# Attention B's norm turned by DMA instead of by TensorE

## The chip, the cores and the metric

The kernel runs on one core of a Trainium2 chip. TensorE (PE in the profile) does matmuls and, with an identity matrix, transposes; VectorE (DVE), ScalarE (ACT) and GpSimd (POOL) do element-wise work; SyncE (SP) issues DMAs, and a DMA can transpose 16-bit data on its way. The engines run side by side and wait for each other on semaphores. The metric is the time of one execution in microseconds (us) on the device; of several runs the median.

## The reference

Four residual layers follow each other on 1024 rows of 512 numbers (two sequences of 512): attention A, a mixture-of-experts FFN, attention B, and the same FFN again. Cut to what matters:

```
x = hidden_states                                  # 2 x 512 x 512
x = x + attn_a(layernorm(x), quantised weights)
x = x + ffn(layernorm(x), gate_w, lora_A, lora_B)
x = x + attn_b(layernorm(x), Wq, Wk, Wv, Wo)
x = x + ffn(layernorm(x), gate_w, lora_A, lora_B)

layernorm(x) = (x - mean(x)) / sqrt(var(x) + eps)
attn_b: q = n @ Wq (32 heads of 16), k = n @ Wk, v = n @ Wv (8 heads of 16),
        rotary embedding of q and k, causal softmax, out @ Wo
```

## The kernel before, in words

The 1024 rows are NT = 8 tiles of 128 rows. All matmuls are made from 16-bit pairs: a value is a high part (its f16 rounding) and a low part (the rest), and a product is three matmuls (high by high, high by low, low by high; `three`, L1253 to L1255). A projection contracts over the 512 columns, so it needs the normalised rows turned: `xt` holds, for each tile, four 128x128 blocks of the high part and four of the low part, columns on the partitions.

A norm of tile t has these steps. DVE takes the statistics (`ln_stats`), POOL the reciprocal root (`ln_rsqrt`, L591), DVE subtracts and scales (`ln_norm`, L1861). From there two ways exist. In the norms of attention A and B (c = 0 and 2) the result goes to `xn`, PE turns it with four f32 transposes into a PSUM bank (`ln_t`, L1262), ACT makes the high part out of the bank (`ln_hi`, L889) and DVE the low part (`ln_lo`, L1871), both straight into `xt`. In the norms of the FFNs (c = 1 and 3) `ln_norm` writes a PSUM bank in row layout, ACT writes the high part and DVE the low part into `rows` (`row_hi`, L897; `row_lo`, L1866; two buffers), and SP turns both with one DMA transpose of 128 x 1024 (`turn_rows`, L500), whose landing PE awaits on `d_rows`.

The work around the change is the projection stage of attention B. The order on every engine is written out by hand. The engines' queues go strictly in order, SP's among them: an instruction that waits holds all behind it. PE does, for t from 0 to 5, the query projection of tile t (`project_q`, 12 matmuls of 512 columns), the transposes of tile t + 2, and the key and value projection (`project_kv`, 12 matmuls of 256 columns); tiles 6 and 7 are cut in halves with the first scores between them. Behind a query projection come, in this order, the rotary products on DVE (`rope_q`, L2267 and L2268), their sum on POOL (`queries_rot`, L819), the high part into `q_stack` on ACT (L1215), the low part on POOL (`queries_low`, L830), and SP's DMA transpose into `qt_b` (`turn_queries`, L519). Keys go the same way with half the columns: products (`rope_k`), sum (`keys_rot`, L824), high part (L1221), low part (`keys_low`, L813), transpose into `kt_b` (`turn_keys`, L523). POOL's order for a tile is `queries_rot(t)`, `keys_low(t - 1)`, `keys_rot(t)`, `queries_low(t)`: the keys' low part of a tile stands behind the sum of the next tile's queries. SP issues the turn of tile t's queries and then that of its keys, behind a wait for `stacks_set`, which POOL sets when it has cleared the stacks (its last memset is L806).

In front of the stage lies the FFN's second half: PE's `second(m)` (12 matmuls of 512 columns per tile), DVE's addition and statistics (`y_stats`), and ACT's and POOL's preparation of attention B's weights (`w_scale` L1140, `w_high` L1144, `w_low` L746; `b_o` is the last).

Of the kernel before, what the change touches and what calls it, by code (L numbers as in the profile page):

```python
# [24 lines left out]
P = 128  # L25
B, S, D = 2, 512, 512
TOK = B * S
NT = TOK // P
ST = S // P
KT = D // P  # L30
# [71 lines left out]

LN_BANK = {0: (0, 1, 0, 1, 6, 1, 6, 6), 2: (2, 3, 2, 3, 2, 3, 2, 3)}
XN_BANK = {1: (3, 2), 3: (4, 3)}

HALF = NT // 2
GATE_BANK = [(7, 4), (5, 2)]
# [102 lines left out]
def build(nc, t_in, out):  # L212
    ctx = ExitStack()
    with ctx:
# [7 lines left out]
        bank = [banks[:, i] for i in range(8)]  # L222
# [5 lines left out]
        xn = sb("xn", [P, 2, D], F32)  # L228
# [187 lines left out]
        d_turned, d_rows = ([sem(f"{n}{i}") for i in range(2)] for n in ("d_turned", "d_rows"))  # L416
# [43 lines left out]

        def rows_landed(c, t):

            return 16 * (HALF * (c // 2) + t // 2 + 1)

        block = ctx.enter_context(nc.Block())
        N_CONST = 3
# [3 lines left out]
        def _(sp):  # L470
# [43 lines left out]
                turn_rows(1, t)  # L514
            for t in range(NT):
                turn_hidden(0, t)
            def turn_queries(t):
                sp.wait_ge(bq_lo, t + 1)
                sp.dma_start_transpose(qt_b[:, :, t * P:(t + 1) * P], q_stack[:, t % 2]).then_inc(d_q[t % 2], 16)  # L519
# [5 lines left out]
            def turn_max(q, c):  # L525
                sp.wait_ge(bsplit_done, 2 * q + c + 1)
                if q >= 2:
                    sp.wait_ge(d_mrows[c][q % 2], 32 * (q // 2))
                sp.dma_start_transpose(m_turned[:, q % 2, c].rearrange("p (i n) -> p i n", n=P),
                                       m_stack[:, q % 2, c].rearrange("p i n -> p (i n)")).then_inc(d_mturn[c], 16)  # L530

# [8 lines left out]

            sp.wait_ge(stacks_set, 2)
            for t in range(NT - 2):
                turn_queries(t)
                turn_keys(t)
            turn_max(0, 0)
# [339 lines left out]
        @block.scalar  # L885
        def _(act):
            def ln_hi(c, t):
                act.wait_ge(xt_ps, NT * (c // 2) + t + 1)
                act.activation(xt_hi[:, :, t * P:(t + 1) * P],  # L889
                               bank[LN_BANK[c][t]][:].rearrange("p (k n) -> p k n", k=KT),  # L890
                               ACT.Copy, scale=X_UP).then_inc(xthi_done, 1)

            def row_hi(c, t):
                act.wait_ge(xn_ready, NT * c + t + 1)
                if c == 3 or t >= 2:
                    act.wait_ge(d_rows[t % 2], rows_landed(c, t) - 16)
                act.activation(rows[:, t % 2, 0], bank[XN_BANK[c][t % 2]][:], ACT.Copy, scale=X_UP).then_inc(xthi_done, 1)  # L897

# [284 lines left out]
            def experts(ph):  # L1183
                c = 1 + 2 * ph
                for t in range(3):
                    h_out(ph, t)
                    row_hi(c, 5 + t)
                h_out(ph, 3)
                gate_exp(ph, 0)
                h_out(ph, 4)  # L1190
                h_out(ph, 5)
                rows_high(ph, 0)
                h_out(ph, 6)
                rows_high(ph, 1)
                gate_exp(ph, 1)
                h_out(ph, NT - 1)
                for t in range(2, NT):
                    rows_high(ph, t)
                    if ph == 0:
                        w, n = beside[t - 2]  # L1200
                        w(n)

            experts(0)

# [15 lines left out]
                rk = rk1[:, i2].rearrange("p (h d) -> p h d", d=B_HD).unsqueeze(2)  # L1220
                act.activation(st[:, :, :, 0], rk.broadcast_to([P, KV_HEADS, 4, B_HD]), ACT.Copy).then_inc(bk_hi, 1)  # L1221

            ln_hi(2, 0)
            ln_hi(2, 1)
            for t in range(NT):
                if t + 2 < NT:
                    ln_hi(2, t + 2)
                stack_high(t)

            for q in range(SETS + 2):  # L1230
# [19 lines left out]
        def _(pe):  # L1250
# [6 lines left out]
            def ln_t(c, t):  # L1257
                pe.wait_ge(xn_ready, NT * c + t + 1)
                if t >= 2:
                    pe.wait_ge(xt_done, NT * c + t - (c > 0 or t != NT - 1))  # L1260
                for k in range(KT):
                    mm = pe.transpose(bank[LN_BANK[c][t]][:, k * P:(k + 1) * P],  # L1262
                                      xn[:, t % 2, k * P:(k + 1) * P], ident[:])
                mm.then_inc(xt_ps, 1)

# [311 lines left out]
            def experts(ph):  # L1577
                c = 1 + 2 * ph
                m0, f0 = ph * 2 * NT, ph * NT
                if ph == 0:  # L1580
                    pe.wait_ge(wlo_done, 5)
                    pe.wait_ge(o_added, NT * (KV_HEADS - 1) + 3)
                for t in range(NT):
                    if t == NT - 1 and ph == 0:
                        pe.wait_ge(redw[1], 3)
                        pe.transpose(bank[PEAK_BANK][:, P:P + 3], w_peaks[0:3], ident[0:3, 0:3]).then_inc(redw[1], 1)
                    pe.wait_ge(d_rows[t % 2], rows_landed(c, t))
                    if t == 1 and ph == 0:
                        pe.wait_ge(o_added, NT * (KV_HEADS - 1) + 6)
                    if t == NT - 3 and ph == 0:  # L1590
                        pe.wait_ge(amaxw_done[1], 3)
                        pe.transpose(bank[PEAK_BANK][0:3, 0:P], amax_w[:, 3:6], ident[:]).then_inc(redw[1], 1)
                    if t == HALF:
                        if ph == 0:
                            pe.wait_ge(o_added, NT * KV_HEADS)
                        else:
                            pe.wait_ge(y_added, 2 * NT)
                    e0 = t % HALF * EXPERTS
                    wide(bank[GATE_BANK[ph][t // HALF]][:, e0:e0 + EXPERTS], t, "gate", EXPERTS).then_inc(g_ps, 1)
                    if t >= 2:  # L1600
                        pe.wait_ge(h_done, f0 + t - 1)
                    wide(bank[t % 2][:], t, "lora_a", D).then_inc(h_ps, 1)
                if ph == 0:
                    pe.wait_ge(wlo_done, 9)
                for t in range(NT):
                    if ph == 0 and t == NT - 1:
                        ln_t(2, 0)
                    second(m0 + t, "lora_b")
                if ph == 0:
                    ln_t(2, 1)  # L1610

            experts(0)

# [57 lines left out]
            def project_q(t, first=True, last=True):  # L1671


                if first:
                    pe.wait_ge(xt_done, 2 * NT + t + 1)
                    if t >= 2:
                        pe.wait_ge(bq_mul, t - 1)
                mm = wide(bank[t % 2][:], t, "b_q", D, range(0 if first else KT // 2, KT if last else KT // 2))
                if last:
                    mm.then_inc(bq_ps, 1)  # L1680
# [7 lines left out]

            for t in range(NT - 2):
                project_q(t)  # L1690
                ln_t(2, t + 2)
                project_kv(t)
            pe.wait_ge(zeros_done, 5)
            project_q(NT - 2, last=False)
# [134 lines left out]
        def _(dve):  # L1829
# [22 lines left out]

            def ln_norm(c, t):
                i = NT * c + t
                if c % 2:
                    dve.wait_ge(xt_done, i - 1)
                elif t >= 2:
                    dve.wait_ge(xt_ps, NT * (c // 2) + t - 1)
                dve.wait_ge(ln_rstd, i + 1)
                to = bank[XN_BANK[c][t % 2]][:] if c % 2 else xn[:, t % 2]  # L1860
                dve.tensor_scalar(to, x[:, t], mv[:, t, 0:1], rstd[:, t:t + 1], ALU.subtract,  # L1861
                                  ALU.mult).then_inc(xn_ready, 1)

# [5 lines left out]
            def ln_lo(c, t):  # L1869
                dve.wait_ge(xthi_done, NT * c + t + 1)  # L1870
                dve.scalar_tensor_tensor(out=xt_lo[:, :, t * P:(t + 1) * P],  # L1871
                                         in0=bank[LN_BANK[c][t]][:].rearrange("p (k n) -> p k n", k=KT),
                                         scalar=X_UP, in1=xt_hi[:, :, t * P:(t + 1) * P], op0=ALU.mult,
                                         op1=ALU.subtract).then_inc(xt_done, 1)

# [352 lines left out]
            def experts(ph):  # L2228
# [10 lines left out]
                for t in range(NT):  # L2239
                    if t + 3 < NT:  # L2240
                        rows_low(ph, t + 3)
                    if ph:
                        y_add(m0 + t, t, c_ffn)
                        continue
                    if t == NT - 1:
                        ln_norm(2, 1)
                        ln_lo(2, 0)
                        ln_norm(2, 2)
                        ln_lo(2, 1)
                    y_stats(m0 + t, t, c_ffn, 2)  # L2250
                    if t == NT - 3:
                        ln_norm(2, 0)

            experts(0)
# [67 lines left out]
            for t in range(NT - 2):  # L2322
                rope_q(t)
                rope_k(t)
                ln_lo(2, t + 2)
                if t + 3 < NT:
                    ln_norm(2, t + 3)
            b_max(0, 0, 3)
# [148 lines left out]
```

## Time and profile before

| | us |
|---|---|
| runs | 952.43, 947.94, 952.37 |
| median | 952.37 |
| profiled execution, its own time | 950.79 |
| span of the profile in it | 949.1 |

| engine | busy us | share |
|---|---|---|
| PE | 912.1 | 96% |
| DVE | 771.8 | 81% |
| ACT | 598.8 | 63% |
| POOL | 618.9 | 65% |

The span runs from the first to the last instruction; the rest of the execution's time (1.7 us) lies around it. The stage of this case is from about 716 to 755 us of the span. A start time is counted from the span's start. A timeline row of the trace gives start, duration, engine, line, operation, output and inputs, count, and in brackets how long the engine had been idle and who released it.

### The profile page before, as it was taken

The numbers are of one execution on the slowest core, as the hardware profiler recorded it, in microseconds if no ns is written. First come the engines' busy times: TensorE is split into PE (matmuls) and PEld (weight loads), VectorE is DVE, ScalarE is ACT, GpSimd is POOL, SyncE is SP. The second block draws the span as 40 slices with busy tenths as digits, with TensorE's granted clock in tenths as the row PEclk, the third lists the DMA queues.
The fourth block names the chain that finished last, engine by engine and source line by source line (L and its number), as shares of the span: only waits on it lengthen the run. The fifth ranks groups of instructions, "written<-read, shape, count | busy, mean of one in ns | idle before, by whom it ended". The sixth has DMA issues, their size and how long they took to land.

```text
span 949.1 us, 19791 instructions
## 1 busy us (share of the span) xinstructions
PE 912.1 (96%) x6698; PEld 487.6 (51%) x6698; DVE 771.8 (81%) x1812; ACT 598.8 (63%) x1323; POOL 618.9 (65%) x668
## 2 busy tenths in 40 slices
PE   5889999999999999999999999999999989999998
PEld 3445555555555555545555555554445534444543
DVE  6888887887887788788788878898878879996764
ACT  4677666676667567666576756646463469997331
POOL 4788876968777687687777777822368744553211
PEclk9999999999999999999999999999999999999999
DMA  9177376484665556647557465464332943121145
GB/s 339 51 182 173 87 185 145 63 211 107 122 186 88 144 116 157 144 86 199 117 101 190 83 144 144 87 175 84 76 82 55 163 80 64 42 43 24 23 86 159
DMA packets 256005, 114.10 MB, mean 120 GB/s; under 512 B 244144, under 2 KB 244784, under 8 KB 251312
## 3 DMA queue, kind: packets, MB, share of 16 engines
q1 hardware_dynamic: 246416, 70.42, 39.1%
q10 hardware_dynamic: 9504, 42.49, 12.9%
q8 instruction: 60, 0.98, 0.4%
q14 instruction: 25, 0.20, 0.1%
HBM read 49.84 MB, written 2.10 MB: 55 GB/s over the span
## 4 chain that ended last, share of the span: by engine, by line
PE 76%; DVE 10%; ACT 6%; issue 3%; DMA 3%; POOL 1%; SPq 1%; ACTq 0%; DVEq 0%; POOLq 0%
PE bank L1253 16%; PE bank L1255 16%; PE bank L1254 16%; PE bank L1734 4%; PE bank L1352 3%; PE bank L1354 3%; PE bank L1353 3%; PE bank L1372 3%; PE bank L1374 3%; PE bank L1373 3%; ACT bank L989 2%; PE bank L1666 2%; DVE bw_hi L1981 2%; DVE bank L1964 2%; PE bank L1640 2%
## 5 line engine op out<-in xcount | busy, mean ns | idle before, releaser
L622 POOL TENSOR_TENSOR rt<-rt 128x512 f32<-128x512 f32 x80 | 101.6, 1273 | 131.8 <-DVE rt L1949 131.8
L1981 DVE SCALAR_TENSOR_TENSOR bw_hi<-bank,rden,bw_hi 128x128 f16<-128x128 f32 (+3 forms) x256 | 123.3, 544 | 60.9 <-ACT bw_hi L1025 60.9
L989 ACT ACTIVATE bank<-bank,shift,c_score 128x128 f32<-128x128 f32 (+3 forms) x256 | 147.3, 605 | 2.1
L1964 DVE CUSTOM_DVE_ANT_0 bank<-bank,mask_w 128x512 f32<-128x512 f32 (+3 forms) x256 | 117.9, 520 | 21.5 <-PE bank L1354 21.5
L1025 ACT ACTIVATE bw_hi<-bank,rden 128x128 f16<-128x128 f32 (+3 forms) x256 | 114.5, 535 | 22.4 <-DVE rden L1974 22.2
L984 ACT ACTIVATE shift<-smax,c_score 128x4 f32<-128x4 f32 x64 | 19.0, 297 | 155.4 <-DVE smax L1964 155.4
L629 POOL TENSOR_TENSOR arena<-rt,arena 128x512 f16<-128x512 f32 x80 | 92.4, 1158 | 8.6 <-ACT arena L973 7.8
L1253 PE MATMUL bank<-xt,wq_hi 128*128 128x512 f16 x256 | 97.0, 379 | 0.0
L1254 PE MATMUL bank<-xt,wq_hi 128*128 128x512 f16 x256 | 97.0, 379 | 0.0
L1255 PE MATMUL bank<-xt,wq_lo 128*128 128x512 f16 x256 | 97.0, 379 | 0.0
L1253 PE MATMUL bank<-wo_hi,arena 128*128 128x512 f16 x256 | 97.0, 379 | 0.0
L1254 PE MATMUL bank<-wo_lo,arena 128*128 128x512 f16 x256 | 97.0, 379 | 0.0
L1255 PE MATMUL bank<-wo_hi,arena 128*128 128x512 f16 x256 | 97.0, 379 | 0.0
L1006 ACT ACTIVATE pt<-bank,c_score_b 128x512 f32<-128x512 f32 x128 | 79.6, 684 | 15.2 <-PE bank L1666 13.1
L1352 PE MATMUL bank<-arena 128*128 128x512 f16 (+3 forms) x256 | 73.4, 300 | 7.1 <-DVE bw_hi L1981 6.8
L1372 PE MATMUL bank<-bw_lo,arena 128*128 128x512 f16 (+3 forms) x256 | 76.6, 299 | 1.9 <-DMA bw_lo<-bw_hi 1.4
L1373 PE MATMUL bank<-bw_lo,arena 128*128 128x512 f16 (+3 forms) x256 | 76.6, 299 | 0.0
L1353 PE MATMUL bank<-arena 128*128 128x512 f16 (+3 forms) x256 | 76.6, 299 | 0.0
L1354 PE MATMUL bank<-arena 128*128 128x512 f16 (+3 forms) x256 | 73.8, 299 | 0.0
L1374 PE MATMUL bank<-bw_lo,arena 128*128 128x512 f16 (+3 forms) x256 | 73.3, 299 | 0.0
L1947 DVE TENSOR_TENSOR rt<-bank,sin_a 64x512 f32<-64x512 f32 x80 | 55.5, 693 | 16.6 <-PE bank L1255 14.7
L973 ACT ACTIVATE arena<-rt 128x512 f16<-128x512 f32 x80 | 51.3, 645 | 9.9 <-POOL rt L622 9.9
(241 smaller groups left out, 2453.6 us busy)
## 6 DMA issues: line engine op xcount, KB each, us to landing
qcode<-in_q_codes ACTq DMA_DIRECT2D x7, 1024.0 KB, 5.0
qscale<-in_q_scales ACTq DMA_DIRECT2D x7, 1024.0 KB, 7.2
ocode<-in_o_codes ACTq DMA_DIRECT2D x7, 1024.0 KB, 4.9
oscale<-in_o_scales ACTq DMA_DIRECT2D x7, 1024.0 KB, 7.9
kvcode<-in_k_codes ACTq DMA_DIRECT2D x8, 256.0 KB, 7.5
kvcode<-in_v_codes ACTq DMA_DIRECT2D x8, 256.0 KB, 7.9
kvscale<-in_k_scales ACTq DMA_DIRECT2D x8, 256.0 KB, 8.1
kvscale<-in_v_scales ACTq DMA_DIRECT2D x8, 256.0 KB, 8.9
```

What stands on the lines that cost most here:

```text
L989: act.activation(a_rows(i, s), a_rows(i, s), ACT.Exp, bias=shift[:, s % 2, c:c + 1], scale=c_score[:, 0:1], accum_out=bank[3][:, SUMS_AT + ...
L1025: act.activation(p_row[:, s % 2, HI_AT[i]:HI_AT[i] + P_STEP * i + 1:P_STEP], turned_back(i, s), ACT.Copy, scale=rden[:, s % 2, c:c + 1]).t ...
L1253: pe.matmul(out_ap, a_hi, b_hi, start=(k == 0), stop=False)
L1254: pe.matmul(out_ap, a_hi, b_lo, start=False, stop=False)
L1255: return pe.matmul(out_ap, a_lo, b_hi, start=False, stop=(stop and k == n - 1))
L1352: pe.matmul(o_ap, q_hi[:, s, qs], k_hi[:, b, 0:w], start=True, stop=False)
L1353: pe.matmul(o_ap, q_hi[:, s, qs], k_lo[:, b, 0:w], start=False, stop=False)
L1354: mm = pe.matmul(o_ap, q_lo[:, s, qs], k_hi[:, b, 0:w], start=False, stop=True)
L1372: pe.matmul(o_ap, v_hi[:, b, vs], hi, start=(kt == 0), stop=False)
L1373: pe.matmul(o_ap, v_hi[:, b, vs], lo, start=False, stop=False)
L1964: dve.tensor_tensor_reduce(bank[bk][:, o:o + (i + 1) * P], bank[bk][:, o:o + (i + 1) * P], mask_w[:, S - (i + 1) * P:S], 1.0, LOWEST, ALU. ...
L1981: dve.scalar_tensor_tensor(out=p_row[:, s % 2, LO_AT[i]:LO_AT[i] + P_STEP * i + 1:P_STEP], in0=turned_back(i, s), scalar=rden[:, s % 2, c: ...
```

## The change

Attention B's norm (c = 2) goes the way of the FFNs' norms. `ln_norm(2, t)` writes a PSUM bank in row layout, `row_hi` and `row_lo` fill `rows`, SP's `turn_rows(2, t)` turns them into `xt`, and `project_q(t)` waits for `d_rows`. PE's eight calls of `ln_t(2, t)` are gone. In the FFN's tail the first norms move: `ln_norm(2, 0)` one tile earlier, the low parts of tiles 0 and 1 before tiles 6 and 7's statistics, and ACT makes the high part of tile 0 between `rows_high(7)` and the last weight step. On SP tiles 0 and 1 are turned after the FFN's last hidden turn, tile 2 behind the wait for `stacks_set`, and tile t + 2 ahead of the queries and keys of tile t.

```diff
-LN_BANK = {0: (0, 1, 0, 1, 6, 1, 6, 6), 2: (2, 3, 2, 3, 2, 3, 2, 3)}
-XN_BANK = {1: (3, 2), 3: (4, 3)}
+LN_BANK = (0, 1, 0, 1, 6, 1, 6, 6)
+XN_BANK = {1: (3, 2), 2: (2, 3), 3: (4, 3)}
@@ SyncE
+            turn_rows(2, 0)
+            turn_rows(2, 1)
...
                 if q >= 2:
                     sp.wait_ge(d_mrows[c][q % 2], 32 * (q // 2))
+                elif c == 0:
+                    sp.wait_ge(d_rows[q], rows_landed(2, NT - 2 + q))
...
             sp.wait_ge(stacks_set, 2)
             for t in range(NT - 2):
+                turn_rows(2, t + 2)
                 turn_queries(t)
                 turn_keys(t)
@@ ScalarE, FFN tail and attention B
                     if ph == 0:
+                        if t == NT - 1:
+                            row_hi(2, 0)
                         w, n = beside[t - 2]
                         w(n)
+                if ph == 0:
+                    row_hi(2, 1)
...
-            ln_hi(2, 0)
-            ln_hi(2, 1)
             for t in range(NT):
                 if t + 2 < NT:
-                    ln_hi(2, t + 2)
+                    row_hi(2, t + 2)
                 stack_high(t)
@@ TensorE
                 for t in range(NT):
-                    if ph == 0 and t == NT - 1:
-                        ln_t(2, 0)
                     second(m0 + t, "lora_b")
-                if ph == 0:
-                    ln_t(2, 1)
...
                 if first:
-                    pe.wait_ge(xt_done, 2 * NT + t + 1)
+                    pe.wait_ge(d_rows[t % 2], rows_landed(2, t))
...
             for t in range(NT - 2):
                 project_q(t)
-                ln_t(2, t + 2)
                 project_kv(t)
@@ VectorE
+                    if t == NT - 2:
+                        row_lo(2, 0)
+                        ln_norm(2, 1)
                     if t == NT - 1:
-                        ln_norm(2, 1)
-                        ln_lo(2, 0)
                         ln_norm(2, 2)
-                        ln_lo(2, 1)
+                        row_lo(2, 1)
                     y_stats(m0 + t, t, c_ffn, 2)
-                    if t == NT - 3:
+                    if t == NT - 4:
                         ln_norm(2, 0)
...
                 rope_q(t)
                 rope_k(t)
-                ln_lo(2, t + 2)
+                row_lo(2, t + 2)
                 if t + 3 < NT:
                     ln_norm(2, t + 3)
```

SP's queue at the start of the stage before; `qt_b<-q_stack` turns a tile's queries, `kt_b<-mt` its keys, `mt<-m_stack` is the FFN's hidden turn.

```order
L500 DMA_TRANSPOSE xt<-rows 128x8x128 x8
L510 DMA_TRANSPOSE mt<-m_stack 128x8x128 x8
L519 DMA_TRANSPOSE qt_b<-q_stack 128x16x128
L523 DMA_TRANSPOSE kt_b<-mt 128x8x128
L519 DMA_TRANSPOSE qt_b<-q_stack 128x16x128
L523 DMA_TRANSPOSE kt_b<-mt 128x8x128
```

The same place of SP's queue after the change; `xt<-rows` behind the hidden turns are the new ones.

```order
L500 DMA_TRANSPOSE xt<-rows 128x8x128 x8
L510 DMA_TRANSPOSE mt<-m_stack 128x8x128 x8
L500 DMA_TRANSPOSE xt<-rows 128x8x128 x3
L521 DMA_TRANSPOSE qt_b<-q_stack 128x16x128
L525 DMA_TRANSPOSE kt_b<-mt 128x8x128
L500 DMA_TRANSPOSE xt<-rows 128x8x128
L521 DMA_TRANSPOSE qt_b<-q_stack 128x16x128
L525 DMA_TRANSPOSE kt_b<-mt 128x8x128
```

Tiles 0 to 2 now go ahead of the first queries, and tiles 3 to 7 each stand behind the keys of the tile three below.

ScalarE at the end of the FFN and the start of the stage, before (`bw_hi<-oscale` is the high part of the weight `b_o`, `bv` the values of a tile):

```order
L1172 ACTIVATE m_stack<-hs 128x512
L1144 ACTIVATE bw_hi<-oscale 128x2048
L889 ACTIVATE xt<-bank 128x4x128 x3
L1208 ACTIVATE bv<-bank 128x8x16
L1215 ACTIVATE q_stack<-rq 128x32x32
```

The same place after:

```order
L1177 ACTIVATE m_stack<-hs 128x512
L902 ACTIVATE rows<-bank 128x512
L1149 ACTIVATE bw_hi<-oscale 128x2048
L902 ACTIVATE rows<-bank 128x512 x2
L1217 ACTIVATE bv<-bank 128x8x16
L1224 ACTIVATE q_stack<-rq 128x32x32
```

The first of attention B's high parts now stands ahead of the weight's high part, which so waits for the first norm.

## Rows read from the trace of the kernel before

**Rows 1.** The page: the span, and the shares of the last chain.
```profile
span 949.1 us, 19791 instructions
...
PE 76%; DVE 10%; ACT 6%; issue 3%; DMA 3%; POOL 1%; SPq 1%; ACTq 0%; DVEq 0%; POOLq 0%
```

**Rows 2.** Chain that ended last, 690 to 780 us: start, us, what.
```profile
693.74 2.70 DMA mt<-m_stack
...
740.46 0.44 PE bank L1262 x4
...
755.14 0.48 DVE rq L2267 x2
```

**Rows 3.** PE's timeline: second half's start, then query projections of tiles 3, 4, 5, 7.
```profile
696.57 0.38 PE L1253 MATMUL bank<-lora_b_hi,mt 128*128 128x512 f16 x1 [1.98 <-DMA mt<-m_stack]
...
733.37 0.38 PE L1253 MATMUL bank<-bw_hi,xt 128*128 128x512 f16 x1
...
737.71 0.38 PE L1253 MATMUL bank<-bw_hi,xt 128*128 128x512 f16 x1
...
742.05 0.38 PE L1253 MATMUL bank<-bw_hi,xt 128*128 128x512 f16 x1
...
751.86 0.39 PE L1253 MATMUL bank<-bw_hi,xt 128*128 128x512 f16 x1
```

**Rows 4.** SP's timeline, turns of queries 0, keys 0, queries 1, keys 4.
```profile
729.29 2.02 SPq L519 DMA_TRANSPOSE qt_b<-q_stack  x1
731.36 1.64 SPq L523 DMA_TRANSPOSE kt_b<-mt  x1
733.05 1.82 SPq L519 DMA_TRANSPOSE qt_b<-q_stack  x1
...
748.19 1.24 SPq L523 DMA_TRANSPOSE kt_b<-mt  x1
```

**Rows 5.** POOL's timeline: last memset; then sum of queries 5, keys 4, queries 5.
```profile
725.35 0.31 POOL L806 MEMSET mt<- 128x256 f32 x1
...
746.27 1.26 POOL L819 TENSOR_TENSOR rq<-rq 128x512 f32<-128x512 f32 x1 [0.72 <-DVE rq L2268]
747.50 0.67 POOL L813 TENSOR_TENSOR mt<-hs,mt 128x256 f16<-128x256 f32 x1
...
748.70 1.16 POOL L830 TENSOR_TENSOR q_stack<-rq,q_stack 128x512 f16<-128x512 f32 x1
```

**Rows 6.** DMA from 729 to 752 us: queue's packets, MB, share; issues with us to landing.
```profile
q1 hardware_dynamic: 16397, 4.12, 100.8%
...
qt_b<-q_stack SPq DMA_TRANSPOSE x6, 4.5
kt_b<-mt SPq DMA_TRANSPOSE x5, 3.5
```

**Rows 7.** Line L500, all sixteen row turns of the FFNs' norms: issue ns, landing us.
```profile
L500 SPq DMA_TRANSPOSE xt<-rows x16: 1231/1233/1369, 662.1 to 914.9; - x16
...
DMA to landing us min/median/max: 3.0/3.1/4.8
```

**Rows 8.** Windows: us, busy of PE, PEld, DVE, ACT, POOL, PEclk, DMA share, GB/s.
```profile
697.00:700.60 3.60, 3.60 (x10) 1.27 (x9) 1.82 (x5) 3.60 (x4) 1.04 (x1) 0.53 0.42 94
700.60:704.00 3.40, 3.40 (x17) 1.57 (x16) 2.85 (x5) 2.43 (x4) 2.56 (x3) 1.00 0.34 77
```

**Rows 9.** Lines L1861, L897, L1866 from 655 to 700 us: ns min/median/max.
```profile
L1861 DVE TENSOR_SCALAR bank<-x,mv,rstd x8: 805/810/815, 659.9 to 683.1; 128x512 f32<-128x512 f32 x8
...
L897 ACT ACTIVATE rows<-bank x8: 597/597/598, 660.7 to 684.6; 128x512 f16<-128x512 f32 x8
...
L1866 DVE SCALAR_TENSOR_TENSOR rows<-bank,rows x8: 682/688/692, 661.4 to 685.3; 128x512 f16<-128x512 f32 x8
```

**Rows 10.** Timelines of DVE and ACT in the FFN's tail.
```profile
714.13 0.15 DVE L1851 TENSOR_SCALAR mv<-mv 128x1 f32<-128x1 f32 x1
...
710.09 1.89 ACT L1144 ACTIVATE bw_hi<-oscale 128x2048 f16<-128x2048 f32 x1
```

More of the change, by code:

```diff
@@ L461, in rows_landed @@
         def rows_landed(c, t):
-            return 16 * (HALF * (c // 2) + t // 2 + 1)
+            return 16 * (HALF * (c - 1) + t // 2 + 1)
         block = ctx.enter_context(nc.Block())
@@ L887, in ln_hi @@
             def ln_hi(c, t):
-                act.wait_ge(xt_ps, NT * (c // 2) + t + 1)
+                act.wait_ge(xt_ps, t + 1)
                 act.activation(xt_hi[:, :, t * P:(t + 1) * P],
-                               bank[LN_BANK[c][t]][:].rearrange("p (k n) -> p k n", k=KT),
+                               bank[LN_BANK[t]][:].rearrange("p (k n) -> p k n", k=KT),
                                ACT.Copy, scale=X_UP).then_inc(xthi_done, 1)
@@ L894, in row_hi @@
                 act.wait_ge(xn_ready, NT * c + t + 1)
-                if c == 3 or t >= 2:
+                if c > 1 or t >= 2:
                     act.wait_ge(d_rows[t % 2], rows_landed(c, t) - 16)
@@ L1261, in ln_t @@
                 for k in range(KT):
-                    mm = pe.transpose(bank[LN_BANK[c][t]][:, k * P:(k + 1) * P],
+                    mm = pe.transpose(bank[LN_BANK[t]][:, k * P:(k + 1) * P],
                                       xn[:, t % 2, k * P:(k + 1) * P], ident[:])
@@ L1854, in ln_norm @@
                 i = NT * c + t
-                if c % 2:
+                if c:
                     dve.wait_ge(xt_done, i - 1)
                 elif t >= 2:
-                    dve.wait_ge(xt_ps, NT * (c // 2) + t - 1)
+                    dve.wait_ge(xt_ps, t - 1)
                 dve.wait_ge(ln_rstd, i + 1)
-                to = bank[XN_BANK[c][t % 2]][:] if c % 2 else xn[:, t % 2]
+                to = bank[XN_BANK[c][t % 2]][:] if c else xn[:, t % 2]
                 dve.tensor_scalar(to, x[:, t], mv[:, t, 0:1], rstd[:, t:t + 1], ALU.subtract,
@@ L1871, in ln_lo @@
                 dve.scalar_tensor_tensor(out=xt_lo[:, :, t * P:(t + 1) * P],
-                                         in0=bank[LN_BANK[c][t]][:].rearrange("p (k n) -> p k n", k=KT),
+                                         in0=bank[LN_BANK[t]][:].rearrange("p (k n) -> p k n", k=KT),
                                          scalar=X_UP, in1=xt_hi[:, :, t * P:(t + 1) * P], op0=ALU.mult,
```

## The prediction

> **What bounds the kernel now.** I read the page first. PE makes 76% of the chain that ended last [rows 1], so the kernel is bound by TensorE over its whole length, and what counts in one stage is what PE waits for there. The chain in the stretch of the change shows that: it goes through PE's matmuls of the projections without a break, the four transposes of each tile are in it with 0.44 us [rows 2], and it passes to DVE at 755.14, after the last query projection. PE's timeline gives the beat: the query projections of tiles 3, 4 and 5 start at 733.37, 737.71 and 742.05, 4.34 us apart, and that of tile 7 at 751.86 [rows 3]. Without its transposes a tile would take PE 4.34 - 0.44 = 3.90. I call S(t) the start of tile t's query projection, and compare S(7) before and after: all that follows (scores, maxima, softmax) hangs on it.
>
> The second resource is the queue that receives new work. SP turns a tile's queries in 2.02 or 1.82 us and its keys in 1.64, back to back at the start [rows 4], about 3.7 of the 4.34. From 729 to 752 us that queue's packets fill all 16 DMA engines (100.8% of them, 4.12 MB in 23 us) [rows 6]. This is a stage in which DMA has almost nothing to spare, and the change puts 5 more transposes between those of queries and keys.
>
> **What the change removes.** 32 f32 transposes on PE, eight times 0.44 = 3.5 us, all in the chain. ACT's and DVE's two steps stay one for one at about the same cost (0.60 and 0.69 us in the FFN's form [rows 9]), and the norm into PSUM takes 0.81; DVE and ACT have idle time in the stage (DVE is released by PE in each tile), so I take nothing for them. The bounds for that are 0 and, if DVE's fell into the chain, 0.1 a tile.
>
> **The start of the stage.** The statistics of tile 4 end at 714.13 + 0.15 = 714.3 [rows 10]. The norm of tile 0 follows (0.8), then ACT's high part (0.6, ready 715.7), while DVE does tile 5's addition and statistics (1.8, to 716.9); the low part is done at 717.5, SP turns, and it lands 3.1 later [rows 7] at 720.6. S(0) was 720.1, so 0.5 later, though PE is ready a microsecond earlier. ACT's high part of `b_o` (1.89 us) began at 710.09 [rows 10] and now stands behind the first row part: it ends near 717.5 instead of 712, and POOL's low parts of it, its last three reciprocal roots and memsets end some 0.3 us later than 725.35 + 0.31 [rows 5], near 726.0. That releases tile 2's turn, so S(2) = 726.0 + 3.1 = 729.1, as before within 0.1. The first queries are ready 0.3 later too. Up to here nothing is won or lost.
>
> **Tile 3, where the wait begins.** Queries 0 were turned at 729.29, keys 0 at 731.36 and queries 1 at 733.05 [rows 4]; with 0.3 more the third place is free at 733.35, and there tile 3's rows are turned, though they have been ready since about 730.6. A 256 KB transpose behind another lands after 3.5 us here (the keys' median; the rows' own median in quiet stretches is 3.1) [rows 6, 7], and PE starts 0.13 after a landing (693.74 + 2.70 to 696.57) [rows 2, 3]. S(3) = 733.35 + 3.5 + 0.13 = 737.0, against 733.37 before. PE has finished tile 2 at 729.1 + 3.9 = 733.0 and stands still for 4 us.
>
> **The loop over tiles.** Tile t + 3's rows are issued behind tile t's keys. Those keys wait for POOL's `keys_low(t)`, which stands behind `queries_rot(t + 1)`, which needs the query projection of tile t + 1. Before, from S(5) = 742.05 the sum of queries 5 ran at 746.27, the keys' low part of tile 4 at 747.50, and SP issued keys 4 at 748.19 [rows 3, 4, 5]: 6.14 us. So S(t + 3) = S(t + 1) + 6.14 + 1.24 (the keys' issue) + 3.2 (landing, between 3.1 and 3.5) + 0.13 = S(t + 1) + 10.7, that is 5.35 us a tile instead of 4.34. A second bound is the queue itself: 3.7 + 1.23 [rows 7] = 4.9 a tile. The loop is the tighter. With the clock full: S(4) = 741.8 (rows issued at 738.15 behind queries 1 and keys 1), S(5) = 737.0 + 10.7 = 747.7, S(6) = 752.5, S(7) = 758.4. Against 751.86 that is +6.6.
>
> **PE's clock.** After the idle 1.98 us before 696.57 the granted clock in 697.0 to 700.6 was 0.53, half speed, and 1.00 behind it [rows 3, 8]; 3.6 x 0.47 = 1.7 us of PE's work was lost. The Trainium skill says the same of a matmul loop that waits for DMAs ("TensorE: Matmul & The Clock Gate", section on HAM oscillation): each such wait can send the array to half clock again. That rule speaks for a loss at every long wait; by it the stage would pay twice. The idle times ahead of S(3) (4 us) and S(5) (about 3) are both longer than the 1.98 that sufficed. I take one spell, 1.7 us, since the wait before S(5) shrinks by what S(4) is late; the bounds are 0 and 3.4. It delays query 3's end and so keys 2 and S(5), S(7): on the path. Sum: 950.8 (the profiled execution's own time) + 6.6 + 1.7 = 959.1. The median of the three runs is 1.6 above the profiled execution, by which it would be 960.7; I say 960.
>
> A rule of the Trainium skill speaks against the queue as a bound. "DMA: Bandwidth & Descriptors", Specifications, gives the fabric a ceiling of 435 GB/s; an estimate from it for the 1.05 MB of queries, keys and rows is 2.4 us a tile, so the rows would cost nothing in bandwidth. The trace disagrees for transposes: at a full share it moved 4.12 MB in 23 us, 180 GB/s, and one 256 KB turn holds the queue 1.23 us, 213 GB/s. No number above uses the rule.
>
> **Rivals.**
> - *Faster: PE sets the beat.* If SP reached each row turn before PE needed it, each tile would take 3.9 and the 3.5 us would be won: 950.8 - 3.7 = 947.1. The point from which it decides: tile 3's rows must be issued by 729.4, that is before queries 0 or right behind them. For it speaks that rows are ready 2 us earlier than SP comes to them; against it that the order on SP is fixed and that queries 0 and keys 0 hold the queue until 733.
> - *Only the queue's capacity counts.* If keys were ready when SP comes to them, rows would follow each other by 4.9: the issue of tile 7's is 733.35 + 4 x 4.9 = 753.0, S(7) = 756.6, +4.7, 955.5. Against it speak the 6.14 us from a projection to the keys' issue, measured without any wait of SP before it.
> - *One wait, then hidden.* The wait before S(3) costs 3.6 and later tiles run at 3.9, so that 4 x 0.44 comes back: +1.9, 952.7, no difference. It needs the loop to be shorter than 7.8 us for two tiles, and the three rows that make it give 10.7.
> - *Two or more clock spells*, 962.5 and above.
>
> **How the numbers follow.** The loop with one or two spells, or none: 0.70 (957.4 to 962.5), more than that 0.05, the queue's capacity alone 0.13, hidden again 0.06, faster 0.06. A change of under 0.5% (4.8 us) can't be told from none in measurements of this kernel. Against the median 952.4, slower by more than that is from 957.1: the first two cases and a part of the third, 0.80; same 0.14; faster 0.06. The range of 8 in 10 is 954.5 to 964.
>
> **What would show it.** Right: after the third turn of the stage SP's timeline reads rows, queries, keys in turn; PE's largest releaser in the stage is the DMA `xt<-rows`, with some 4 us before tile 3's projection and PE idle at tile 5; a period near 5.3 for tiles 3 to 7; S(7) near 758 to 760; a stretch of half clock after S(3); everything behind tile 7 shifted alike. Wrong: S(3) at 733 would refute the queue order's role; a period of 4.9 with SP never idle would put the queue's capacity in the loop's place; waits on PE elsewhere (bank or statistics) would mean another bound.

## The result, and the profile after

| | before | after |
|---|---|---|
| median of the runs, us | 952.4 | 962.75 |
| lowest to highest, us | 947.94 to 952.58 | 961.75 to 964.93 |
| profiled execution, us | 950.79 | 964.93 |
| span of the profile, us | 949.1 | 963.2 |

The kernel before has four runs here, a fourth of 952.58 beside the three above. The changed kernel is slower, by a ratio of 1.0113 with a 95% interval of 1.0093 to 1.0133. The page after, first PE's busy time, then the shares of the last chain and its costliest lines:

```profile
PE 917.1 (95%) x6666; PEld 487.5 (51%) x6666; DVE 772.9 (80%) x1812; ACT 599.2 (62%) x1323; POOL 616.8 (64%) x668
...
PE 74%; DVE 13%; ACT 5%; DMA 3%; issue 3%; SPq 1%; ACTq 0%; POOL 0%; DVEq 0%; POOLq 0%
PE bank L1260 15%; PE bank L1261 15%; PE bank L1262 15%; PE bank L1736 4%; PE bank L1359 3%; PE bank L1361 3%; PE bank L1360 3%; PE bank L1379 3%; PE bank L1381 3%; PE bank L1380 3%; PE bank L1643 2%; ACT bank L994 2%; PE bank L1669 2%; DMA xt<-rows 2%; DVE bw_hi L1983 2%
```

PE has 32 instructions fewer (6698 before) and is busy 5 us longer, because more of them ran at half clock (mean granted clock of the execution 0.984, before 0.995); and the landing of `xt<-rows` has come into the chain with 2%, beside the shares before in [rows 1].

The profiled executions can't be subtracted as they stand. SP's first hidden turn, in front of everything that the change touches, was at 693.74 before [rows 2] and is at 698.84 after:

```profile
698.84 20.00 SPq L510 DMA_TRANSPOSE mt<-m_stack  x8
```

These 5.1 us lie in identical instructions. In the traces of all the kernels of this study that moment lies between 693.63 and 698.84, so it varies from run to run. I therefore count inside the stage, from the query projection of tile 2. PE's timeline after, query projections of tiles 2 to 7 (start, us, engine, line, operation, idle time before it and who ended it):

```profile
734.15 0.39 PE L1260 MATMUL bank<-bw_hi,xt 128*128 128x512 f16 x1 [0.26 <-DMA xt<-rows]
...
741.76 0.61 PE L1260 MATMUL bank<-bw_hi,xt 128*128 128x512 f16 x1 [3.54 <-DMA xt<-rows]
...
748.40 0.38 PE L1260 MATMUL bank<-bw_hi,xt 128*128 128x512 f16 x1
...
755.75 0.39 PE L1260 MATMUL bank<-bw_hi,xt 128*128 128x512 f16 x1 [3.28 <-DMA xt<-rows]
...
761.09 0.38 PE L1260 MATMUL bank<-bw_hi,xt 128*128 128x512 f16 x1 [1.27 <-issue]
...
766.61 0.39 PE L1260 MATMUL bank<-bw_hi,xt 128*128 128x512 f16 x1
```

The same start of tile 2 before, to which tiles 3, 4, 5 and 7 of [rows 3] belong:

```profile
729.04 0.38 PE L1253 MATMUL bank<-bw_hi,xt 128*128 128x512 f16 x1
```

From tile 2's projection to tile 7's it was 751.86 - 729.04 = 22.82 us before and is 766.61 - 734.15 = 32.46 after: 9.64 more, which is the measured difference of the medians (10.35) but for 0.7. Two long waits for row turns, 3.54 and 3.28 us, lie in it. SP's timeline says why they are there; rows of tile 3, rows, queries and keys around tiles 4 to 7, after:

```profile
738.12 1.34 SPq L500 DMA_TRANSPOSE xt<-rows  x1
...
743.54 1.33 SPq L500 DMA_TRANSPOSE xt<-rows  x1
744.91 2.15 SPq L521 DMA_TRANSPOSE qt_b<-q_stack  x1
750.46 1.89 SPq L525 DMA_TRANSPOSE kt_b<-mt  x1
752.39 1.31 SPq L500 DMA_TRANSPOSE xt<-rows  x1
...
757.58 1.34 SPq L500 DMA_TRANSPOSE xt<-rows  x1
...
763.18 1.34 SPq L500 DMA_TRANSPOSE xt<-rows  x1
```

Tile 3's rows were complete at 735.07 (DVE's low part) and turned at 738.12. Between 747.06 and 750.46 SP waits for tile 2's keys, and tile 5's rows stand behind them. POOL's timeline shows that these keys were ready just when SP issued them, and only after an idle time of 6.57 us in which POOL waited for tile 3's rotary products:

```profile
748.53 1.26 POOL L824 TENSOR_TENSOR rq<-rq 128x512 f32<-128x512 f32 x1 [6.57 <-DVE rq L2271]
749.76 0.67 POOL L818 TENSOR_TENSOR mt<-hs,mt 128x256 f16<-128x256 f32 x1
```

The windows around tile 3's wait give the clock (last three numbers: granted clock, DMA share, GB/s; a granted clock of 1.00 is 2.4 GHz, one of 0.50 is 1.2 GHz):

```profile
736.00:740.50 4.50, 2.22 (x17) 1.37 (x14) 3.18 (x8) 2.87 (x5) 3.89 (x6) 1.00 1.10 205
740.50:747.30 6.80, 5.54 (x15) 2.11 (x16) 0.20 (x1) 1.44 (x3) 1.33 (x2) 0.50 1.05 194
747.30:750.00 2.70, 2.70 (x19) 1.75 (x18) 2.55 (x8) 0.44 (x2) 1.47 (x2) 0.99 0.59 110
```

TensorE has half speed for 6.8 us, from the idle time into tile 3's projection, which with its keys and values takes 748.40 - 741.76 = 6.64 us instead of 3.9. The slow projection is also what made tile 2's keys late: they were issued 750.46 - 741.76 = 8.70 us after the start of tile 3's projection, where the same step took 6.14 before.

### The profile page after: what moved, and what is told of

It is laid out like the page before. It is cut to its first block, busy times and chain, and to the rows that moved or that the text cites. A ratio compares the mean times of both kernels' runs of the same rounds, so it can differ in the third digit from the quotient of the medians.

```text
span 963.2 us, 19741 instructions
## 1 busy us (share of the span) xinstructions
PE 917.1 (95%) x6666; PEld 487.5 (51%) x6666; DVE 772.9 (80%) x1812; ACT 599.2 (62%) x1323; POOL 616.8 (64%) x668
## 4 chain that ended last, share of the span: by engine, by line
PE 74%; DVE 13%; ACT 5%; DMA 3%; issue 3%; SPq 1%; ACTq 0%; POOL 0%; DVEq 0%; POOLq 0%
PE bank L1260 15%; PE bank L1261 15%; PE bank L1262 15%; PE bank L1736 4%; PE bank L1359 3%; PE bank L1361 3%; PE bank L1360 3%; PE bank L1379 3%; PE bank L1381 3%; PE bank L1380 3%; PE bank L1643 2%; ACT bank L994 2%; PE bank L1669 2%; DMA xt<-rows 2%; DVE bw_hi L1983 2%
```

## The experiments

"Tile 2 to 7" is the time from tile 2's query projection to tile 7's; "turn to turn" is the mean distance of neighbouring row turns on SP, from the first that stands behind a tile's keys. Both are read in one profiled execution of each kernel; the medians are of 4 to 10 executions. The lengthening of "tile 2 to 7" and that of the median agree within 2.5 us, so the medians alone don't tell kernels 1 or 2 us apart. Each kernel ran beside the kernel before (medians 951.1 to 952.3).

| kernel | tile 2 to 7 | turn to turn | median us | ratio to before, 95% interval |
|---|---|---|---|---|
| before | 22.82 | | 952.4 | 1 |
| after | 32.46 | 6.27 | 962.75 | 1.0093 to 1.0133 |
| rows ahead | 30.63 | 5.56 | 959.12 | 1.0043 to 1.0096 |
| keys early | 29.89 | 5.46 | 957.65 | 1.0047 to 1.0088 |
| kept busy | 30.76 | 5.85 | 958.31 | 1.0036 to 1.0079 |
| three by DMA | 22.81 | | 950.74 | 0.9972 to 1.0005 |
| rows ahead + keys early | 30.27 | 5.55 | 957.39 | 1.0044 to 1.0087 |
| rows ahead, half the bytes | 28.16 | 5.40 | 957.37 | 1.0042 to 1.0098 |
| keys early, half the bytes | 28.43 | 5.38 | 956.63 | 1.0037 to 1.0065 |
| keys early, kept busy | 29.58 | 5.49 | 955.89 | 1.0032 to 1.0061 |
| keys early, two turns | 35.09 | 6.66 | 964.99 | 1.0086 to 1.0155 |
| five by DMA | 28.68 | | 955.53 | 1.0018 to 1.0054 |
| four by DMA, ahead | 24.52 | | 952.09 | 0.9983 to 1.0014 |

**Rows ahead of queries on SP.**

```diff
             sp.wait_ge(stacks_set, 2)
+            turn_rows(2, 2)
             for t in range(NT - 2):
-                turn_rows(2, t + 2)
+                if t + 3 < NT:
+                    turn_rows(2, t + 3)
                 turn_queries(t)
                 turn_keys(t)
```

> Edit: on SyncE tile t+3's rows are turned ahead of the queries and keys of tile t, instead of behind them (tile 2's still first). Bytes and instructions are those of the changed kernel. Theory A (the place in SyncE's order makes the wait: rows that are ready stand behind keys that wait for the next tile's projection, and the long waits halve TensorE's clock): no wait of more than 1 us before tile 3's projection, no stretch of half clock in the stage, tile spacing set by the queue's 4.9 us at most, tile 7's projection 1.5 to 3 us later than in the kernel before instead of 9.6; in all 953.5 to 956. Rival B (the DMA engines' capacity for the added bytes makes all of the loss): the same bytes cost the same, 961 to 964. Rival C (the loss comes from DVE's and ACT's new order in the FFN's tail): unchanged, 961 to 964.

Tile 3's wait was gone, as expected, and with it the fall of the clock there. But the time came down by 3.6 us and not by 8: 959.1, outside the expectation, with tile 7's projection 7.8 us later than before and not 1.5 to 3. SP's timeline of this kernel is without a gap, and its turns are longer (five of six queries' turns took 2.15 to 3.31 us; in the kernel before five of the six took 1.82 to 2.02 and one 3.21):

```profile
736.04 1.34 SPq L500 DMA_TRANSPOSE xt<-rows  x1
737.42 1.81 SPq L521 DMA_TRANSPOSE qt_b<-q_stack  x1
739.28 1.90 SPq L525 DMA_TRANSPOSE kt_b<-mt  x1
741.22 1.34 SPq L500 DMA_TRANSPOSE xt<-rows  x1
742.60 3.31 SPq L521 DMA_TRANSPOSE qt_b<-q_stack  x1
745.96 1.34 SPq L525 DMA_TRANSPOSE kt_b<-mt  x1
747.35 1.32 SPq L500 DMA_TRANSPOSE xt<-rows  x1
```

The expectation also left out that the scores need the keys, which come out of the same full queue: the first scores waited for those of tile 3. The granted clock fell there, to 0.50 from 755.5 to 758.5, where no spell at all was expected.

```profile
754.92 0.39 PE L1645 MATMUL bank<-kt_b,qt_b 64*128 64x512 f16 x2 [2.49 <-DMA kt_b<-mt]
```

Tile 6's projection, which stands ahead of these scores, started 21.02 us after tile 2's (17.34 before, 26.94 in the changed kernel); so of the 7.8 us that were left, 3.7 had arisen by then and 4.1 arose between tiles 6 and 7. Theory A, that the order makes the loss by itself, fell here. Rival B, that capacity makes all of it, didn't hold either, since 3.6 us did come back.

**Keys' low part early on POOL.**

```diff
                 queries_rot(t)
-                if t:
-                    keys_low(t - 1)
                 if t == NT - 1:
+                    keys_low(t - 1)
                     b_split(0, 1)
...
                 queries_low(t)
+                if t < NT - 2:
+                    keys_low(t)
```

> Edit: on GpSimd the low part of tile t's keys (tiles 0 to 5) is made right behind tile t's queries' low part, instead of behind the sum of tile t+1's queries. SyncE's order is that of the changed kernel. Theory A says the loop rows(t+1) - projection(t+1) - keys low(t) - rows(t+3) is cut at the keys: tile 3 still waits (some 3.5 us, its rows stand behind queries 0 and keys 0) and the clock still falls there, but tile 5 doesn't wait any more (under 1 us) and tile 7's projection comes about 2.5 us earlier than in the changed kernel: 959 to 961. Rival B (capacity alone): no difference, 961.5 to 964.

Tile 7 came 2.57 us earlier, as expected, and the median is lower than expected (957.65 against 959 to 961). A wait of 2.05 us before tile 5 remained, where under 1 was expected: with the loop cut the turns follow each other without a gap, at 5.46 us a tile. The clock behaved otherwise than expected too: after tile 3's wait of 3.31 us it stayed at 1.00, and it fell to 0.50 from 748.5 to 751.5, after the wait of 2.05. So the 2.57 us hold two things, the loop that was cut and a spell of half clock that moved; the last of the runs with TensorE kept busy takes them apart.

**PE kept busy while it waits.**

```diff
                 if first:
+                    keep_busy(CTX_BANK, {3: 22, 4: 6, 5: 10, 6: 5}.get(t, 0))
                     pe.wait_ge(d_rows[t % 2], rows_landed(2, t))
```

> Edit: TensorE runs idle matmuls (128x384, into a bank that nobody reads) ahead of its wait for the rows of tiles 3, 4, 5 and 6 (22, 6, 10 and 5 of them), so that it waits busy. Everything else is the changed kernel. Theory A with the clock as a cost of its own: the granted clock stays 1.00 in the stage, projection of tile 3 and its keys and values take 3.9 us and not 6.6, the waits for rows stay at the same places, tile 7's projection starts 3 us earlier: 959 to 960.5. Rival (the clock's loss is hidden behind the rows' wait anyway): 962 to 963.

The granted clock was 1.00 over the whole stage (window 735 to 762), and 958.3 is below the changed kernel by 4.4 us and below the expectation. Inside the stage only 1.7 us came back, not 3: the faster projection of tile 3 runs into tile 4's rows (a wait of 1.79 us), which wait for the queue. The idle matmuls have a price too: tile 5's rows, turned at 744.43, landed 3.3 us later, at 747.7, and its projection began at 749.07, behind the ten matmuls. So the clock is a cost of its own, in part hidden behind the turns; in the stage it is worth 1.7 us at least, and about a microsecond more if that delay is counted.

```profile
735.00:762.00 27.00, 24.73 (x173) 13.75 (x172) 14.53 (x35) 10.12 (x17) 14.64 (x19) 1.00 1.03 180
```

```profile
747.44 1.79 PE L1277 MATMUL bank<-mask_w 128*128 128x384 bf16 x10
749.07 0.38 PE L1260 MATMUL bank<-bw_hi,xt 128*128 128x512 f16 x1
```

With tile 3's projection at full clock, SP did not wait for tile 2's keys. They were ready at 742.82, 6.1 us after the start of that projection, and SP came to them at 743.07, behind a queries' turn of 3.24 us; behind one of 2 us it would have waited for about one. SP's first wait for keys (1.8 us) came with tile 3's.

```profile
739.79 3.24 SPq L521 DMA_TRANSPOSE qt_b<-q_stack  x1
743.07 1.31 SPq L525 DMA_TRANSPOSE kt_b<-mt  x1
```

**Only tiles 0 to 2 by DMA.**

```diff
+BY_DMA = 3
@@ SyncE
-                turn_rows(2, t + 2)
+                if t + 2 < BY_DMA:
+                    turn_rows(2, t + 2)
@@ TensorE
                 project_q(t)
+                if t + 2 >= BY_DMA:
+                    ln_t(2, t + 2)
                 project_kv(t)
```

(ACT, DVE and the waits take the matching way per tile.)

> Edit: only the norms of tiles 0, 1 and 2 are turned by DMA; tiles 3 to 7 are turned by TensorE as in the kernel before. Part of the change is undone, so five of the eight row transposes are gone from SyncE's order between queries and keys, and five of TensorE's are back. Theory A: all of the loss lies in tiles 3 to 7, so tile 3's projection starts at the time of the kernel before (within 0.3 us) and the time is that of before, 951 to 953.5. Rival C (the loss, or part of it, comes from the FFN's tail, where DVE's and ACT's order changed and the weight's high part waits): 954 or more.

It took 22.81 us from tile 2 to tile 7, that of before to 0.01. The median, 950.74, is 0.3 below the range and can't be told from that of before. So the FFN's tail, the start of the stage and the first three turns cost nothing, which refutes rival C, and gain nothing that these runs can tell. The rows of tiles 2 and 7:

```profile
733.23 0.38 PE L1265 MATMUL bank<-bw_hi,xt 128*128 128x512 f16 x1
...
756.04 0.39 PE L1265 MATMUL bank<-bw_hi,xt 128*128 128x512 f16 x1
```

**Rows ahead and keys early together.** The edit is the sum of the two diffs.

> Edit: both of the two earlier ones together: SyncE turns tile t+3's rows ahead of tile t's queries and keys, and GpSimd makes the keys' low part right behind the queries'. No waiting order is left that keeps a turn back; the bytes are all there. Theory D (formed from the runs before: with the order mended the queue of transposes itself is full, at some 5.45 us for a tile's rows, queries and keys, and that sets the beat): row turns 5.3 to 5.6 apart on average, SyncE's queue without idle time, the first scores still wait for the keys of tile 3, and the time is that of either edit alone, 957 to 959.5. Theory A (order alone makes the loss): with both edits no wait is left and the time comes to 953 to 955.

The median is 957.4, as theory D has it, and no better than the better of the two alone. SP has next to no idle time and rows still follow each other by 5.55. The first scores still wait 1.97 us for the keys of tile 3, and the granted clock fell twice, behind the wait of 2.05 us before tile 5 and behind that one. With the order mended the queue, with the spells that its waits bring, is what is left.

**Half the bytes, in two orders.**

```diff
+            def turn_high(c, t):
+                sp.wait_ge(xt_done, NT * c + t + 1)
+                sp.dma_start_transpose(xt[:, 0, :, t * P:(t + 1) * P],
+                                       rows[:, t % 2, 0]).then_inc(d_rows[t % 2], 16)
```

> Edit: rows ahead on SyncE as before, and of tiles 3 to 7 only the high part (128x512, 128 KB) is turned; attention B's low part of these tiles is left as the FFN's norm wrote it, so part of the computation is left out. Instructions and waits are the same, the added bytes of these five turns are halved. Theory D (bytes through the queue): the beat falls by about 0.6 us a tile, to 4.8, row turns 4.6 to 5.0 apart, and tile 7's projection comes 2.5 to 3.5 us earlier than with rows ahead alone: 955 to 957. Rival E (a turn costs a fixed time in the queue whatever its size): no difference, 958.5 to 960.

> Edit: the keys' low part early on GpSimd, SyncE's order of the changed kernel, and of tiles 3 to 7 only the high part turned (the low part is left out as in the other run of this kind). Theory D (bytes through the queue): row turns 4.6 to 5.0 apart instead of 5.46, tile 7's projection 2.5 to 3.5 us earlier than with the full bytes: 954 to 956. Rival E (fixed time for each turn): no difference from the keys' edit alone, 957 to 958.5. Tile 3 still waits some 3 us in both, since its place in the order is the same.

Theory D missed in both: the distance of row turns fell from 5.56 to 5.40 and from 5.46 to 5.38, not to 4.6 to 5.0. Rival E, no difference, is nearer but not exact: tile 7 came 2.5 and 1.5 us earlier, and the medians, 957.4 and 956.6, lie between the two expectations, 1.8 and 1.0 below those with the full bytes, with runs that overlap. Rows landed after 2.6 us instead of 3.4, which is a part of that; another is that both kernels with the full bytes had a spell of half clock in the stage and both with half the bytes none. So bytes are a small part. What holds the queue shows in SP's timeline and DMA's windows of "keys early, half the bytes": a turn of 128 KB keeps SP 1.27 us, nearly what 256 KB do (1.34), and some 2 us behind its start the DMA engines have little to do for half a microsecond or a whole one (last two numbers: DMA share, GB/s).

```profile
733.29 1.27 SPq L505 DMA_TRANSPOSE xt<-rows  x1
734.61 1.85 SPq L526 DMA_TRANSPOSE qt_b<-q_stack  x1
736.51 1.90 SPq L530 DMA_TRANSPOSE kt_b<-mt  x1
738.45 1.27 SPq L505 DMA_TRANSPOSE xt<-rows  x1
```

```profile
735.00:735.50 0.50, 0.00 (x0) 0.00 (x0) 0.34 (x1) 0.00 (x0) 0.50 (x2) 1.00 0.45 91
735.50:736.00 0.50, 0.10 (x1) 0.11 (x2) 0.00 (x0) 0.44 (x1) 0.44 (x2) 1.00 0.19 38
...
740.50:741.00 0.50, 0.00 (x0) 0.00 (x0) 0.50 (x2) 0.28 (x1) 0.50 (x1) 1.00 0.00 0
```

**Keys early and PE kept busy.** Both diffs, with 22, 6, 8 and 5 idle matmuls.

> Edit: the keys' low part early on GpSimd, and idle matmuls on TensorE ahead of its waits for the rows of tiles 3 to 6 (22, 6, 8 and 5 of them). Theory D with the clock as a cost of its own: the clock stays at 1.00 in the stage, the beat is that of the queue, tile 7's projection 28.5 to 29.5 us after tile 2's (29.9 with the keys' edit alone), and the runs lie closer together, 956 to 957.5. Rival (the clock's spells are a cost on top of the queue's beat even with the keys' edit): 954.5 to 956.

Tile 2 to 7 took 29.58 us, just above the range, with row turns 5.49 apart. The median, 955.89, lies 0.1 below theory D's range and in the rival's (954.5 to 956). The runs lie closer together, as expected (953.9 to 957.3, where "keys early" spread from 955.5 to 960.7). The clock's remaining spells are worth between 0.3 us (by the traces) and 1.8 (by the medians), which these runs can't tell apart.

Four kernels now differ in just two things, the keys' early low part and TensorE kept busy. In the time from tile 2 to 7, the early keys are worth 32.46 - 29.89 = 2.57 us where the clock is free to fall, but 30.76 - 29.58 = 1.18 where TensorE is kept busy; the clock is worth 1.70 with the loop and 0.31 without. So about half of what the loop seemed to cost was the slow projection of tile 3, which makes tile 2's keys late. (Each number is of one profile, and the idle matmuls delayed tile 5 in both kept-busy kernels.) With both causes gone 29.58 - 22.82 = 6.8 of the 9.64 us are still there: tile 3's first wait and the queue's beat.

**The same bytes in two turns.**

```diff
+            def turn_parts(c, t):
+                sp.wait_ge(xt_done, NT * c + t + 1)
+                for i in range(2):
+                    sp.dma_start_transpose(xt[:, i, :, t * P:(t + 1) * P],
+                                           rows[:, t % 2, i]).then_inc(d_rows[t % 2], 16)
...
-                turn_rows(2, t + 2)
+                (turn_parts if t else turn_rows)(2, t + 2)
```

> Edit: on top of the keys' early low part, the rows of tiles 3 to 7 are turned by two transposes each, one of the high part and one of the low part (128 KB each), instead of one of 256 KB. The bytes are the same, the turns five more. Theory F (from the run with half the bytes, whose turns still took SyncE 1.27 us each: a transpose holds SyncE's queue some 1.25 us however small it is, so the beat counts turns as well as bytes): row turns of neighbouring tiles 6.4 to 6.9 us apart instead of 5.46, tile 7's projection 34 to 36 us after tile 2's (29.9 without), 962 to 965. Rival D (only bytes count): no difference from the keys' edit alone, 956.5 to 959.

All is as theory F has it: 6.66 us between tiles, 35.09 from tile 2 to 7, 965.0. Five turns more with the same bytes cost 7.3 us against "keys early" in the medians and 5.2 from tile 2 to 7. A rival, that the DMA engines themselves are full, doesn't fit: from 733 to 757 us their share was 108% in "keys early", 98% with half the bytes and 91% here, where the beat was longest. SP's timeline, each row being two turns:

```profile
735.87 2.58 SPq L507 DMA_TRANSPOSE xt<-rows  x2
742.34 2.58 SPq L507 DMA_TRANSPOSE xt<-rows  x2
748.78 3.38 SPq L507 DMA_TRANSPOSE xt<-rows  x2
756.05 2.59 SPq L507 DMA_TRANSPOSE xt<-rows  x2
762.49 2.58 SPq L507 DMA_TRANSPOSE xt<-rows  x2
```

**Five tiles by DMA.** `BY_DMA = 5`.

> Edit: tiles 0 to 4 are turned by DMA, tiles 5 to 7 by TensorE; SyncE's order of the changed kernel for those that are left. Theory (each row turn between queries and keys costs once the queue is behind; what a wait took isn't given back): tile 3 waits some 3.3 us as in the changed kernel, the clock may fall there (0 to 2.7), tile 4 comes 1 to 1.5 us later still at full clock, and from tile 5 on the beat is the 4.34 of before; tile 7's projection 4.3 to 7.5 us later than in the kernel before: 955.5 to 958.5. Rival (the loss comes from the steady state of all tiles alone, and TensorE makes good an early wait): under 2 us, 951 to 953.

Tile 7 came 5.86 us late, in the range, at 955.5, the lower edge. Tile 3 waited as in the changed kernel, its projection ran at half clock, and neither loss is given back, though from tile 4 on the beat is again 4.34:

```profile
737.30 0.61 PE L1265 MATMUL bank<-bw_hi,xt 128*128 128x512 f16 x1 [3.41 <-DMA xt<-rows]
```

**Four tiles by DMA, all ahead.** `BY_DMA = 4`, and `turn_rows(2, 2)` and `turn_rows(2, 3)` in front of the loop.

> Edit: tiles 0 to 3 are turned by DMA, all four before the first queries, tiles 4 to 7 by TensorE. The best that I see in reach: the fourth row turn costs nothing if it goes ahead, and saves TensorE 0.44 us. Expected: no wait of more than 0.5 us at tile 3, tile 7's projection within 0.5 us of its place in the kernel before, 950 to 952.5, no difference from before that can be measured. Rival (the first queries and keys, turned 1.3 us later, come too late for the first scores): 1 us or more slower.

The median is 952.09, no difference. Tile 3 didn't wait, as expected, but tile 7 came 1.7 us later than before, since the first scores waited for tile 3's keys. That is the rival, in the trace; the time doesn't show it, at an interval of 0.9983 to 1.0014.

```profile
750.88 0.39 PE L1648 MATMUL bank<-kt_b,qt_b 64*128 64x512 f16 x2 [1.62 <-DMA kt_b<-mt]
```

No version beats the kernel before: "three by DMA" and this one can't be told from it.

## Why the prediction was right

The direction and the place were as forecast, and the size within the range: 962.75 against 960 and 954.5 to 964. The cause was right in kind (rows that are ready wait in SP's queue) but wrong in what sets the beat, and the total held in part by luck: two bounds that lay close together stood in for each other. The result also lies just above the 957.4 to 962.5 that the loop's case was given with 0.70, in the strip given 0.05. Step by step:

- *Start of the stage: nothing won or lost.* Right. From the first hidden turn, tile 2's projection stands at 35.31 us after and at 35.30 before; "three by DMA" shows the same (35.35).
- *Tile 3: rows ready, but behind queries 0 and keys 0.* Right. Forecast S(3) = S(2) + 7.9, measured 7.61; the wait was 3.54 against 4.
- *The loop through the keys' low part, 10.7 us for two tiles.* It was there, but not as the tighter bound. From tile 3's projection to tile 5's it took 13.99 us: 8.70 to the issue of tile 2's keys, where 6.14 had been put in, because that projection ran at half clock; then 1.93 for the issue and 3.36 to the start. With TensorE kept busy the forecast's step held (6.1 us until the keys were ready), and SP didn't wait for them. Of the four distances between row turns after, the loop made one, the 8.85 us up to tile 5's; the other three are 5.42, 5.19 and 5.60, with SP's queue full or nearly so.
- *The queue's own beat, 3.7 + 1.23 = 4.9 a tile.* Wrong in size, the term of the sum that was mis-sized: it measured 5.46 ("keys early"), 5.55 and 5.56 with rows ahead. Two things are missing in 4.9: the row turn is 1.34 in a full queue, and queries and keys took 1.98 + 1.83 behind it, with some 0.13 between the three, 5.28 in all; and once in the stretch the queue stood for about a microsecond more. "Four by DMA, ahead" shows it without rows in between: in a full queue, queries and keys alone follow each other by 3.99 us (mean of five). Since loop and queue lay so close (5.35 and 5.46), the sum came out near in spite of that. The rival "only the queue's capacity counts" had +4.7; worked out with 5.46 it would have been +7.0, and "keys early" measured +7.07.
- *One spell of half clock, 1.7 us.* The number of spells was right. The spell lasted 6.8 us, 3.6 at most had been seen before, and cost 2.7 in tile 3's projection. Of the forecast's +6.6 at full clock and +1.7 for the clock, the kept-busy run gives +7.94 and +1.70, or by about a microsecond less and more, since its idle matmuls delayed tile 5. So the 1.3 us between the forecast's +8.3 and the 9.64 of the stage lie in the beat, in the clock or in both. The spell's premise, that a wait of 1.98 us is enough, holds only at times: the FFN's second half begins in all thirteen traces with a wait of 1.98 to 2.01 us, and in four of them (before, after, "three by DMA", "keys early, two turns") half clock followed. It made the way to tile 2's projection 1.6 us longer there (35.3 to 35.4 us from the first hidden turn, 33.7 to 33.8 in the other nine). The wait before tile 5, 3.28 us, was not followed by a spell in the profile after, so the rule of the Trainium skill that each such wait can cost a spell ("TensorE: Matmul & The Clock Gate", HAM oscillation) is borne out by one wait of the two; that it is a cost of its own the kept-busy run shows.
- *The ceiling of 435 GB/s* ("DMA: Bandwidth & Descriptors" of the Trainium skill, Specifications) again didn't describe these transposes: in "keys early" a DMA share near or above 1 moved mostly 180 to 225 GB/s, and 285 to 290 only in the 2 us behind a standstill.
- *Faster: PE sets the beat.* Refuted, and not only by the order: with rows ahead and keys early the queue still doesn't allow 3.9 a tile. Its sum was also off by 0.2: 3.5 us won from 950.8 is 947.3, not 947.1.

## What to carry to other kernels

Before work goes from a busy engine to a DMA queue, add up that queue's issue times in the stretch, turn by turn, against the beat of the engine it feeds: here 3.7 of 4.34 us were used, and 1.34 more could not fit, in any order. Take the issue times in a full queue: the keys' turn took 1.24 us with room and mostly 1.7 to 1.9 right behind the queries', and that is a part of the error in the 4.9. Up to 256 KB a turn counted with its time on the issuing engine and hardly with its bytes, so splitting a transpose costs (512 KB in one turn took 1.7 to 2.0 us, and no larger ones were tried). And where a queue goes in order, ask of each new entry what the entry ahead of it waits for: here that was a later step of the very engine that waits for the new one. Last, cut two suspected causes one at a time and together: here the second cut was worth half as much once the first was made.

## What the runs showed of the hardware

- A DMA transpose of 128 KB kept SP 1.27 us, one of 256 KB of rows 1.34 in a full queue and 1.23 alone; five turns more at the same bytes cost 7.3 us. Worked out from the beats, an estimate: the queue moved 192 GB/s in "keys early" (1.05 MB in 5.46 us), 171 with the rows' bytes halved (0.92 MB in 5.38 us) and 157 with each row turn cut in two.
- In these stretches the queue stood still for about a microsecond once in a while, in all kernels; in the changed kernel near 767.5, behind the stretch that is counted here. Half-microsecond windows of "keys early" show a burst in the share and then almost nothing moved, and a query turn of 3.12 us instead of 2 beside it. The kernel before has the same near 737.5. I didn't find its cause; it stays open.

```profile
745.00:745.50 0.50, 0.50 (x7) 0.46 (x5) 0.50 (x2) 0.00 (x0) 0.00 (x0) 1.00 3.26 161
745.50:746.00 0.50, 0.31 (x3) 0.03 (x1) 0.50 (x3) 0.00 (x0) 0.03 (x1) 1.00 0.95 22
746.00:746.50 0.50, 0.00 (x0) 0.00 (x0) 0.50 (x4) 0.06 (x1) 0.50 (x1) 1.00 0.09 10
```

- The length of one idle time didn't tell whether the clock falls. After 3.54 us of it TensorE ran at half clock (1.2 of 2.4 GHz), 6.8 us in all; after 3.28 us, in the same execution, at full clock. After 3.31 us in "keys early" it ran at full clock and after 2.05 us in the same execution at half, and the same 2.0 us at the start of the FFN's second half were followed by half clock in four traces of thirteen.
